# A one-core transformer block: the setup in another order, and the combine factors scaled on ScalarE

## The reference

```python
mod = (silu(c) @ wmod).reshape(4, 6, 1, 128)      # sa, ca, ga, sb, cb, gb; ga and gb: |.| at least 0.25
h = layernorm(x) * (1 + ca) + sa
x = x + ga * attn(h)
h = layernorm(x) * (1 + cb) + sb
x = x + gb * ffn(h)

def attn(x):                                      # 256 inner channels
    gate, val = split(rmsnorm(x) @ in_w.T + in_b)
    a = dwconv4(val) @ A @ Bm                     # rank 16
    b = silu(dwconv9(val) + sym_b) @ pw.T + pw_b
    y = concat(a @ ha.T + ha_b, b @ hb.T + hb_b) @ fuse.T + fuse_b
    return x + (sigmoid(gate) * y) @ out_w.T + out_b

def ffn(x):                                       # 160 experts of 64, the best 8 for each token
    probs = sigmoid(x @ router.T + expert_bias)
    combine = top-8 weights / (their sum + 1e-9) * 2.5, else 0
    h1 = silu(x @ w_gate[e].T) * combine[:, e]    # every expert is computed
    return sum_e h1 @ w_down[e].T + silu(x @ wgs.T) @ wds.T
```

## Time and profile before

| what | value |
|---|---|
| median of three runs | 552.45 us |
| the profiled execution, its own time | 555.24 us |
| its span (first to last instruction) | 553.1 us |
| TensorE busy | 522.2 us (94%), 2454 matmuls |
| VectorE busy | 484.9 us (88%) |
| ScalarE busy | 417.4 us (75%) |
| Pool busy | 34.1 us (6%) |
| the chain that ended last | 74% TensorE, 12% VectorE, 5% ScalarE, 5% issue |

### The profile page before, as it was taken

One profiled execution on the slowest core, in us unless ns is written; L12 is line 12 of the kernel. 1 busy time (PEld: TensorE's weight loads), 2 busy tenths in 40 slices (PEclk: granted clock), 3 DMA queues, 4 the chain that ended last, 5 costly groups with the idle time before them and its releaser, 6 DMA issues.

```text
span 553.1 us, 7207 instructions
## 1 busy us (share of the span) xinstructions
PE 522.2 (94%) x2454; PEld 246.5 (45%) x2454; DVE 484.9 (88%) x611; ACT 417.4 (75%) x675; POOL 34.1 (6%) x56
## 2 busy tenths in 40 slices
PE   4887889999999999999999999999989999999996
PEld 2543434544434444444444444444434444444442
DVE  4786799999989998799969998789969989999995
ACT  5446887889887886688777885678797877777774
POOL 6011020050000000030000000010000000000000
PEclk9997999999999999999999999999999999999999
DMA  8787274545534665455434665345535865566550
GB/s 263 298 285 309 68 230 150 182 145 171 183 123 152 211 217 176 140 177 196 185 115 164 212 216 183 129 178 193 213 135 172 245 209 209 191 201 218 190 191 19
DMA packets 33467, 102.92 MB, mean 186 GB/s; under 512 B 3732, under 2 KB 9112, under 8 KB 33304
## 3 DMA queue, kind: packets, MB, share of 16 engines
q1 hardware_dynamic: 33432, 102.47, 54.2%
HBM read 99.57 MB, written 2.36 MB: 184 GB/s over the span
## 4 chain that ended last, share of the span: by engine, by line
PE 74%; DVE 12%; issue 5%; ACT 5%; DMA 2%; POOL 2%; SPq 0%; ACTq 0%; DVEq 0%; POOLq 0%
PE bank L1017 23%; PE bank L1019 23%; PE bank L1018 23%; DVE g_all L983 3%; DVE s_all L987 2%; PE bank L1154 2%; ACT g_all L718 1%; PE bank L1164 1%; DVE attw L902 1%; DMA c_all<-combine 1%; ACT s_all L699 1%; DVE st L852 1%; DVE w L840 1%; POOL rstd L524 1%; DMA res<-x_dram 1%
## 5 line engine op out<-in xcount | busy, mean ns | idle before, releaser
L699 ACT ACTIVATE s_all<-bank 128x512 f32<-128x512 f32 x320 | 189.4, 595 | 95.4 <-PE bank L1019 89.2
L983 DVE TENSOR_TENSOR g_all<-s_all,g_all 128x1024 f16<-128x1024 f32 x160 | 195.0, 1219 | 40.2 <-ACT g_all L718 39.8
L987 DVE TENSOR_TENSOR s_all<-s_all,c_all 128x1024 f32<-128x1024 f32 x160 | 194.6, 1216 | 0.2 <-DMA c_all<-combine 0.2
L718 ACT ACTIVATE g_all<-s_all 128x1024 f16<-128x1024 f32 x160 | 168.4, 1053 | 3.8 <-DVE s_all L987 3.7
L1017 PE MATMUL bank<-x_h,w 128*128 128x512 f16 x320 | 121.5, 380 | 7.0 <-ACT s_all L699 7.0
L1017 PE MATMUL bank<-g_all,w 128*128 128x512 f16 x320 | 121.4, 379 | 3.6 <-DVE g_all L983 3.6
L1018 PE MATMUL bank<-g_all,w 128*128 128x512 f16 x320 | 121.4, 379 | 0.0
L1019 PE MATMUL bank<-g_all,w 128*128 128x512 f16 x320 | 121.3, 379 | 0.0
L1019 PE MATMUL bank<-x_l,w 128*128 128x512 f16 x320 | 121.3, 379 | 0.0
L1018 PE MATMUL bank<-x_h,w 128*128 128x512 f16 x320 | 121.3, 379 | 0.0
L1017 PEld LDWEIGHTS bank<-x_h,w 128*128 128x128 f16 x320 | 31.2, 98 | 50.0 <-ACT s_all L699 14.3
(11 more groups left out here) (217 smaller groups left out, 374.2 us busy)
## 6 DMA issues: line engine op xcount, KB each, us to landing
c_all<-combine SPq DMA_DIRECT2D x160, 512.0 KB, 3.8
w<-w_dram SPq DMA_DIRECT2D x20, 512.0 KB, 10.4
s_all<-mats_dram SPq DMA_DIRECT2D x1, 1152.0 KB, 7.3
res<-x_dram SPq DMA_DIRECT2D x4, 256.0 KB, 7.8
combine<-cT SPq DMA_DIRECT2D x4, 256.0 KB, 3.9
out_dram<-res SPq DMA_DIRECT2D x3, 256.0 KB, 2.9
attw<-symT_dram SPq DMA_DIRECT2D x1, 576.0 KB, 8.5
c_all<-symT_dram SPq DMA_DIRECT2D x1, 576.0 KB, 8.1
```

The lines of the kernel that those rows point to most:

```text
L699: a(sr[J % SRING][:, q * L:(q + 1) * L], U[q][:], ACT.Silu, scale=1.0 / ES).then_inc(s["s_done"], 1)
L718: a(gh[n % GRING], sr[n % SRING], ACT.Copy).then_inc(s["hi_set"], 1)
L983: e.tensor_tensor(gl[n % GRING], sr[n % SRING], gh[n % GRING], ALU.subtract).then_inc(s["lo_set"], 1)
L987: e.tensor_tensor(sr[J % SRING], sr[J % SRING], cr[J % CRING], ALU.mult).then_inc(s["gm"], 1)
```

## The change

- The fold copies move from VectorE to ScalarE (`setup(13)`), as do, for chunks 1 to 3, the scalings of the combine factors (`norm`, four activations, each counted on `cn_set`; the turns on TensorE wait for one tile at a time). Chunk 0 keeps the scaling on VectorE.
- Of the matrices' load three loads are made (in_w; the folds' first operands; fuse). The load of chunk 1 stands ahead of fuse, those of chunks 2 and 3 become one, behind the others; shared weights come in one load (`rsd`). Of the weights' pieces five instead of six are loaded ahead of the row write (EARLY), and the rest only behind the wait for it (`setup(22)`).
- The steps of `walk` are ordered anew up to the loop. VectorE does `sym(0)` right behind `winf`; `gates` comes as `setup(15)` ahead of the first tap; statistics of chunk 1, router halves and `base0` come between the taps; the norm of chunk 1 ahead of y of chunk 0. TensorE does `fold2` ahead of `fold1`, and `fold3` and `wb` behind convolution and gate. ScalarE does silu and tanh of chunk 0 ahead of the copies of `fold3` and `wb`.
- Pool writes its zeros at the beginning; half of its copies stand ahead of the first statistics.
- The columns of gains are made in bank U1 and no longer in TB.
- READY is 7 instead of 8; piece 6 is split as the first thing of the loop; the statistics of chunks 2 and 3 stand ahead of the loop.

The diff, cut to its core; the lists of loads and of `walk` are given in short:

```diff
-EARLY = 6
-READY = 8
+EARLY = 5
+READY = 7
+SOON = 6
 REST: 32: ("sum",), + 33: ("norm",), 34: ("cT",)
@@ walk, in the new order (the old one is in the listing above)
+  setup(0) stat nb setup(1) t1a t1b hm ha setup(2) square setup(9) rms setup(10) setup(4) setup(14)
+  hi low setup(12) setup(5) turn hnT setup(6) val z setup(15) tap0 setup(20) zh setup(13) zl zmv
+  setup(22) conv0:0:9 | 1:stat | setup(8) tap1 base0 tap2 gate setup(3) | 1:nb | tap3..tap8 silu0
+  | 1:t1a 1:t1b | tanh0 tanh1 setup(7) silu1 | 1:hm 1:ha | ya0 ya1 yb0 yb1 | 1:square | wo base1
+  | 1:rms | setup(19) gy0 | 1:hi 1:low | gy1 | 1:turn 1:hnT | o0 o1 setup(21) | 1:z 1:zh | x2 bn
+  rstd2 | 1:zl | setup(11) | 1:zmv 1:conv0:0:6 | split_hi(0) table nb2 split_lo(0) t2a t2b
+  split_hi(1) turn2 | 1:conv0:6:9 | xh split_lo(1) xl logit shup prob ss | 1:silu0 1:conv1:0:5 |
+  max swap cw sum split_hi(2) split_hi(3) cT cT_sb | 1:conv1:5:9 | c_out split_lo(2) split_lo(3)
+  piece(4, 6) | 2:stat 1:silu1 | split_lo(6); then duo(0), split_hi(6), ...; 2:nb at d = 1
@@ SP
 load_chunk(0); wmod
-mat[:, 0:NM]; symT part 0; idf; consts; outT; rows; frow; load_chunk(1..3); symT part 1; rsg; sdf
+mat[:, 0:2 * DI]; mat[:, 2 * DI:NFUSE]; symT part 0; idf; consts; load_chunk(1); mat[:, NFUSE:NM];
+frow; rows; outT; symT part 1; rsd; chunks 2 and 3
                     sp.dma_start(rowd.rearrange("o (b j) -> (o b) j", b=B - 1), row4[1:B]).then_inc(s["row_out"], 16)
-                    weights(EARLY, EARLY + 2)
+                elif n == 22:
                     sp.wait_ge(s["row_out"], 16)
...
-                    weights(EARLY + 2, PIECES)
+                    weights(EARLY, PIECES)
@@ ScalarE
+                elif n == 10:                       # win_h, was in setup(5)
+                elif n == 14:                       # wz_h, was in setup(5)
+                elif n == 21:
+                    taps_hi(1)
+                elif n == 13:
+                    act.wait_ge(s["fold1"], 1)
+                    a(pool_d[:, 0:P + DI], Y[:, 0:P + DI], ACT.Copy)
+                    a(jbc[:, DS:DS + 1], Y[:, 384:385], ACT.Identity, bias=v("hb_b")).then_inc(s["fold1_sb"], 1)
...
+                elif n == "norm":
+                    act.wait_ge(s["rs_set"], c + 1)
+                    act.wait_ge(s["cw_set"], c + 1)
+                    for t in range(NT):
+                        a(cw[:, t, :], cw[:, t, :], ACT.Copy, scale=rs[:, t:t + 1]).then_inc(s["cn_set"], 1)
@@ VectorE
-                elif n == 3:
-                    dve.wait_ge(s["fold1"], 1)
-                    e.tensor_copy(gmat, Y[:, 0:P])
-                    e.tensor_copy(qmat, Y[:, P:P + DI])
...
+                elif n == 9:
                     dve.wait_ge(s["winf_set"], 1)
                     sym(0)
...
-                    e.tensor_tensor(cw[:], cw[:], bc(rs[:], E), ALU.mult).then_inc(s["cn_set"], 1)
+                    if c == 0:
+                        e.tensor_tensor(cw[:], cw[:], bc(rs[:], E), ALU.mult).then_inc(s["cn_set"], 1)
@@ TensorE
-                    pe.wait_ge(s["cn_set"], c + 1)
                     pe.wait_ge(s["pr_set"], 2 * c + 2)
                     for t in range(NT):
+                        pe.wait_ge(s["cn_set"], (c - 1) * NT + t + 2 if c else 1)
                         last = turn(A4[:, t * P:(t + 1) * P], cw[:, t, 0:P], idf[:])
```

More of the change, by code:

```diff
@@ L74 @@
     17: ("t2a",), 18: ("t2b",), 20: ("turn2",), 22: ("xh",), 24: ("xl",), 26: ("logit", "shup"),
[L75 removed]
+    27: ("prob",), 28: ("ss",), 29: ("max",), 30: ("swap",), 31: ("cw",), 32: ("sum",), 33: ("norm",), 34: ("cT",), 35: ("cT_sb", "c_out"),
 }
@@ L122, in walk @@
     att(0, "square")
-    setup(3)
+    setup(9)
     att(0, "rms")
+    setup(10)
     setup(4)
+    setup(14)
     att(0, "hi")
     att(0, "low")
+    setup(12)
     setup(5)
@@ L133, in walk @@
     att(0, "z")
+    setup(15)
     att(0, "tap0")
-    att(0, "tap1")
+    setup(20)
     att(0, "zh")
+    setup(13)
     att(0, "zl")
     att(0, "zmv")
+    setup(22)
     att(0, "conv0:0:9")
-    setup(20)
-    for i in range(2, KS):
+    att(1, "stat")
+    setup(8)
+    att(0, "tap1")
+    att(0, "base0")
+    att(0, "tap2")
+    att(0, "gate")
+    setup(3)
+    att(1, "nb")
+    for i in range(3, KS):
         att(0, f"tap{i}")
-    setup(7)
     att(0, "silu0")
-    att(0, "silu1")
-    att(1, "stat")
-    att(0, "gate")
+    att(1, "t1a")
+    att(1, "t1b")
     att(0, "tanh0")
     att(0, "tanh1")
+    setup(7)
+    att(0, "silu1")
+    att(1, "hm")
+    att(1, "ha")
     att(0, "ya0")
@@ L153, in walk @@
     att(0, "yb1")
-    att(0, "base0")
-    setup(9)
-    att(1, "nb")
+    att(1, "square")
     att(0, "wo")
-    att(1, "t1a")
-    att(1, "t1b")
-    setup(10)
-    split_hi(0)
     att(0, "base1")
+    att(1, "rms")
+    setup(19)
     att(0, "gy0")
+    att(1, "hi")
+    att(1, "low")
     att(0, "gy1")
-    att(1, "hm")
-    att(1, "ha")
-    att(1, "square")
-    split_hi(1)
-    att(1, "rms")
+    att(1, "turn")
+    att(1, "hnT")
     att(0, "o0")
     att(0, "o1")
+    setup(21)
+    att(1, "z")
+    att(1, "zh")
     att(0, "x2")
@@ L174, in walk @@
     att(0, "rstd2")
-    att(1, "hi")
-    att(1, "low")
-    att(1, "turn")
-    att(1, "hnT")
+    att(1, "zl")
+    setup(11)
+    att(1, "zmv")
+    att(1, "conv0:0:6")
+    split_hi(0)
+    att(0, "table")
     att(0, "nb2")
+    split_lo(0)
     att(0, "t2a")
     att(0, "t2b")
-    setup(11)
-    split_lo(0)
+    split_hi(1)
+    att(0, "turn2")
+    att(1, "conv0:6:9")
+    att(0, "xh")
     split_lo(1)
-    setup(8)
-    att(1, "z")
-    att(1, "zh")
-    att(1, "conv0:0:3")
-    att(0, "turn2")
-    att(1, "zl")
-    att(1, "zmv")
-    att(0, "xh")
-    att(0, "table")
     att(0, "xl")
-    att(1, "conv0:3:6")
     att(0, "logit")
@@ L204, in walk @@
     att(0, "sum")
-    att(1, "conv1:0:4")
-    att(1, "silu0")
     split_hi(2)
     split_hi(3)
-    split_lo(2)
     att(0, "cT")
     att(0, "cT_sb")
+    att(1, "conv1:5:9")
     att(0, "c_out")
+    split_lo(2)
     split_lo(3)
-    piece(4, 6)
-    att(1, "conv1:4:9")
+    piece(4, SOON)
+    att(2, "stat")
     att(1, "silu1")
-    piece(6, 8)
+    for i in range(SOON, READY):
+        split_lo(i)
     ready = READY
@@ L221, in walk @@
             duo(c * DUOS + d)
+            if (c, d) == (0, 0):
+                for i in range(SOON, READY):
+                    split_hi(i)
             if d == LAG and c:
@@ L238, in walk, with build @@
     end(B - 1)
-def build(nc, x, vecs, mats, wmod_d, outT_d, consts, rows, frow_d, symT, rsgT, sdT, idf_c, w_d, out):
+def build(nc, x, vecs, mats, wmod_d, outT_d, consts, rows, frow_d, symT, rsgT, idf_c, w_d, out):
     rowd = nc.dram_tensor("rows_mod", (1, (B - 1) * MODC), F32, kind="Internal").ap()
@@ L1000, in end @@
                                     res[:, tiles, :], ALU.add).then_inc(s["fin"], 1)
-            def att_(c, n):
-                if (c, n) == (0, "low"):
-                    gates()
-                att(c, n)
-            walk(setup, att_, nothing, split_lo, duo, end)
+            walk(setup, att, nothing, split_lo, duo, end)
         @block.tensor
@@ L1054, in setup @@
                     last.then_inc(s["sc_ps"], 1)
+                elif n == 12:
+                    for q in range(ML):
+                        mm(Y[:, 0:P], m("haT", q * P, P), bm4[:, q, :], start=(q == 0), stop=(q == ML - 1))
+                    for q in range(ML):
+                        mm(Y[:, P:P + DI], m("hbT", q * P, P), m("pw", q * DI, DI), start=(q == 0), stop=(q == ML - 1))
+                    for q in range(ML):
+                        last = mm(Y[:, 384:385], m("hbT", q * P, P), v("pw_b", q), start=(q == 0), stop=(q == ML - 1))
+                    last.then_inc(s["fold1"], 1)
                 elif n == 3:
                     pe.wait_ge(s["fold1_sb"], 1)
+                    pe.wait_ge(s["ld_fuse"], 16)
                     pe.wait_ge(s["one_set"], 1)
```

112 lines of the change are left out of this document (55 added, 57 removed).

## The result

In the first comparison the changed kernel took 548.5 us (median of four executions, 547.62 to 549.0) beside 552.62 us for the kernel before (552.18 to 553.63): a ratio of 0.9921, 95% interval 0.9902 to 0.994. Forecast were 543.7 and a range of 540.9 to 547.6. The sign was right, the size too large. Later comparisons, on two chips, gave a larger gain: 554.38 us is the median of 88 executions of the kernel before (551.4 to 557.95), 547.85 that of twelve of the changed kernel (546.03 to 548.77). On the one chip the medians were 554.42 and 547.91, ratio 0.9883 [0.9854, 0.9912], on the other 554.14 and 546.59, ratio 0.9865 [0.9833, 0.9897].

The account below looks back on a forecast made before the run. TensorE bounds most of the loop, VectorE its start, so everything hangs on VectorE's first low half behind the setup chain. Setup -9.6 and loop +0.9 gave -8.7 us, taken off the median 552.45: 543.7, range 540.9 to 547.6.

Parts of the forecast that it names:

- Bound, setup up to the taps: Setup chain sets VectorE's first low half and all behind it; first tap at 19.0, 5.2 us earlier.
- From the taps to the gated product, and o: Setup: out projection (o) begins at 37.4, against 39.37, and takes 1.8 at full clock; o's end gains 3.8 us.
- The power of Pool: Chunk 1's rms: beside VectorE work Pool's power takes 2.00 us, adding 1.35; untouched, out projection would begin at 36.7.
- Rival A: Clock: TensorE falls to 1.2 GHz before the out projection (1.85 us) or earlier (1 to 2.5); 545.5 to 548; chance 0.22.
- signs of being wrong: First low half moves under 6 us, out projection still 3.6, VectorE waits for taps or gains, or loop waits grow over 2.
- From o to the low half: Factors turned at 55.6, not 63.39; then 11.5 us to the first low half at 67.1, late landing 0 to 1.
- In the loop: Norm's activations on ScalarE cost 0.4 for chunk 3 and 0.25 each for chunks 1 and 2: +0.9; extra piece 0.
- rival B: VectorE's saved factor scaling counts (norm -0.8 instead of +0.9) and Pool is not slowed: 541.5; chance 0.10.
- C: Loop: ScalarE's hold in norm is not covered, each of three costing 1.5 to 3.3 us; 547 to 552; chance 0.10.
- Rival D: Setup: SP's wait for the row write delays the gains' broadcast for chunk 1's hm; slower, 554 to 557; chance 0.03.
- The sum: -9.6 before the loop and +0.9 in it: -8.7, giving 546.5 from the profiled execution, 543.7 from the median.
- the 3.5 for the turn: From out projection to turned factors: the turn no longer stands behind convolution taps at half clock, a gain of 3.5 us.

Follow-up runs that it names:

- before: Profiled execution of the kernel before, unaltered, from which the prediction was worked out: 555.24 us.
- after: First profiled execution of the changed kernel, unaltered: 549.0 us.
- e3_after: The changed kernel unaltered, run again: median 546.59 us, ratio 0.9865 to the kernel before; its profiled execution took 546.03 us.
- a0_after: The changed kernel unaltered, for more executions: median 547.91 us, ratio 0.9883 to the kernel before.
- b2_oldqueue: The changed kernel with SP's old order of loads, six pieces ahead of the row write and two more ahead of the broadcast: 549.57 us, ratio 0.9914.
- a2_norm_dve: The changed kernel with the combine factors of all chunks scaled on VectorE again: 548.04 us, ratio 0.9879.
- b0_before: The kernel before, unaltered, run again for more executions: 554.29 us, ratio 1.0.
- e1_warm_two: The kernel before with unread matmuls in two TensorE idle gaps, ahead of the out projection and of chunk 1's turns: 552.3 us, ratio 0.996.
- e2_warm_three: The kernel before with unread matmuls ahead of the out projection, chunk 1's turns and the first fold: 552.43 us, ratio 0.9968.
- d4_pool_late: The changed kernel with Pool's zeroing behind its copies, and all of these behind the first statistics: 550.36 us, ratio 0.9927.
- d2_warm: The changed kernel with one matrices load, first duos' loads waiting only for the first factor store, six unread matmuls ahead of chunk 1's turns: 547.98 us.

## Why the prediction was wrong

**Bound, setup up to the taps: right.** The first tap came at 18.94 and 18.63 where wmod landed at 5.40 and 5.09 (before 5.17), 19.0 forecast. In after it came at 20.36, 1.73 later than in e3_after, and wmod had landed 1.74 later, which no term had.

**From the taps to the gated product, and o: right, with one size off.** o began at 37.02 to 38.73 (37.4 forecast) and took 2.05 in most traces (1.8 forecast). The power of Pool took 2.00 in after (at 34.39, beside VectorE's product of two SBUF operands, L784 at 34.17), as L524 did in the earlier trace rows, and the trace so agrees with what was taken from the Trainium skill, SBUF — State Buffer, "Who interferes with whom". From hm to the end of hi it was 6.72 us, 6.74 forecast. (That o would begin at 36.7 without this term doesn't follow from the sum, which gives 36.05.) Rival A came true in some executions: o took 3.54 in a0_after, 1.49 longer (1.85 forecast), and 3.78 in b2_oldqueue. So one of the signs of being wrong, an o of still 3.6, was there in part of the executions.

**From o to the low half: right.** Turned factors at 55.0 in e3_after, 56.7 in after and 56.8 in a0_after (55.6 forecast); then 11.51 and 11.47 to L1011, and 12.72 in after (11.5 forecast, with 0 to 1 us for a late landing). L1011 at 66.51, 68.29 and 69.43; forecast 67.1.

**In the loop: the number right, its cause not.** 0.7 us, and 0.2 more between the last matmul and the end of the execution (5.05 before, 5.25 in a0_after): 0.9, the value taken. But the prediction had it from norm alone, and a2_norm_dve without norm on ScalarE takes 474.36 and not 473.5. That the sizes agree is luck. Of rival B's 0.82 us three times, some 0.15 in all is what the traces show; C's hold never cost more than 0.24 a chunk. Rival D wasn't there: SP's wait for the row write ended well ahead of hm, and b2_oldqueue, with more pieces ahead of it, has a wait of 1.44 us there.

**The sum: this is the step that failed.** The -8.7 was worked out against one execution of 555.24 us. For that scale it gives 546.5, and three profiled executions took 546.03, 547.86 and 549.0. The prediction then took the same 8.7 off the median of 552.45, "2.8 lower". But the kernel before varies by 6.5 us with nothing changed, and a saving that is worked out on one of its slower executions can't be taken off the quicker ones whole. The miss of 4.8 (548.5 less 543.75) is thus, as a sum, 2.8 for the changed base and 2.0 for what the four executions of the changed kernel took above 546.5. Of the latter wmod's landing, a slow o and the factors' landing are seen in traces.

Why the base can't be changed so is in part argued. Several terms are time at 1.2 GHz in that one execution: 1.85 of o's 3.8, and of the 3.5 for the turn some 2.5, an estimate from its twelve matmuls of z and convolution every 0.43 us in place of 0.215. Filling two idle gaps takes 1.8 us off the median, so such time is in the median too. An execution of 552.45 probably has less of it: the twelve of the 88 that had a mean clock of 0.9955 or more took 551.4 to 553.8. But the mean clock alone doesn't order the executions. Fifteen at 0.994 took 552.4 to 557.95, the slowest of all among them, and the clock column misses slow stretches at the start. No trace was taken of the kernel before unaltered at 552 us.

A better base wouldn't have been the whole cure. Beside 554.38, 8.7 off gives 545.7, and the changed kernel took 547.85. Its gain was 6.5 us on the one chip and 7.55 on the other; only there does the interval, 0.9833 to 0.9897, still hold 8.7 (0.9843).

That the first four executions were ones with little time at half clock is only likely: 26 of the 88 later ones took 553.63 or less, so four of four would be rare by chance, and what was different then stays open. So does what makes the landing of wmod or of the second factors late in one execution and not in the next.

## What to carry to other kernels

Work out a change on the profiled execution, but before taking it off the median ask of each term whether it is work or clock: a term that is half-clock time counts only so far as the median has it, so the forecast has two ends, with it and without. Look at what varies between executions of the kernel before first; in the traces here it was the setup alone. Read the clock from the durations and the spacing of like matmuls as well as from its column. When a loss has the size that was forecast, undo its supposed cause before calling it that. An engine that is 6% busy can hold the chain to the first tap, and here its zeroing fitted in where it waited for its first load.

## What the runs showed of the hardware

- The same kernel took 551.4 to 557.9 us in 65 executions on one chip and 552.26 to 557.95 in 23 on another, at mean clocks of 0.978 to 0.997. Which stretches are at 1.2 GHz changes: o at 0.50 in before and 1.00 in b0_before; 20 to 24 at 1.00 in before and 0.77 in b0_before. Ahead of them TensorE had been idle: 2.69 us before the folds, 2.27 before o, 3.35 before chunk 1's turns in b0_before. In e1_warm_two, with two of them filled, the mean was 1.00 in the profile.
- A mean clock of 1.00 doesn't mean that all ran at 2.4 GHz. Executions of e1_warm_two with that mean took 551.94 to 554.08, and in the profiled one of them, 553.11, the matmuls up to 25 us have the durations of 1.2 GHz (1.91 for four of 128x256, 1.03 in e2_warm_three). After, a0_after and e3_after have their folds at 1.91 too, with a column of 1.00.
- Pool's copy of one column took 0.17 us in after, at 2.93, and 1.31 in d4_pool_late, where it began just behind a VectorE product of two SBUF operands and ended with it:

```profile
10.97 1.35 DVE L783 TENSOR_TENSOR attw<-attw,s_all 128x1152 f32<-128x1152 f32 x1
11.05 1.31 POOL L526 COPY c_all<-vec 128x1 f32<-128x1 f32 x1
```

- The power of four columns took 1.04 us in after where VectorE was idle (at 5.58), 2.00 where it began inside a product of 1.35 with two SBUF operands (at 34.39), and 1.21 and 1.29 at 23.77 and 13.98.
- The second load of factors, 512 KB issued with three more of its size, kept its product waiting by 0 us in e3_after, 0.40 in d2_warm, 0.47 in b2_oldqueue, 1.60 in after and 2.05 in d4_pool_late. In the kernel before it was 0.19 and, in b0_before, 1.31.
